# A feed-forward stage computed as seven block products instead of eight, on 1024 tokens at a time

## The reference

```
x = x + layernorm(attention(layernorm(x)))         # one head of width 256, no mask
x = x + layernorm(ffn(layernorm(x)))
ffn(z) = (silu(z @ W_gate.T) * (z @ W_up.T)) @ W_down.T      # W_gate, W_up: 2752 x 1024, W_down: 1024 x 2752
```

## Time and profile before

| | |
|---|---|
| median of 3 runs | 1849.88 us (1849.65 to 1850.52) |
| span of the profiled execution, first to last instruction | 1848.4 us; its own time is not given apart, so the median is 1.5 us above it |
| PE busy | 98% of the span |
| DVE busy | 45% |
| ACT busy | 26% |
| POOL busy | 9% |
| DMA | 199.73 MB, 108 GB/s over the span |
| mean granted clock of TensorE | 0.997 |

### The profile page before, as it was taken

The page is one execution under the profiler, slowest core; times in us unless marked ns, Lnnn a source line. Parts: engine busy times, 40 slices in busy tenths (PEclk is TensorE's granted clock), DMA queues, the critical chain, the costliest instruction groups (busy, mean ns, idle before and its releaser), DMA issues.

```text
span 1848.4 us, 22492 instructions
## 1 busy us (share of the span) xinstructions
PE 1819.5 (98%) x8408; PEld 1511.6 (82%) x8408; DVE 835.0 (45%) x1205; ACT 481.2 (26%) x725; POOL 162.8 (9%) x184
## 2 busy tenths in 40 slices
PE   7999999999999999999999999999999999999997
PEld 5788888888888888888888888888888888888886
DVE  7865766685333442244344423444343234433323
ACT  3233433342222222222222222222222122222221
POOL 4420211221000000011000000110000001000001
PEclk9999999999999999999999999999999999999999
DMA  6311111142222323323324224332232323323231
GB/s 264 114 68 58 45 68 68 68 159 103 101 103 91 136 80 123 128 102 113 125 91 153 74 102 158 114 113 92 110 138 70 146 99 132 113 110 119 98 123 48
DMA packets 36026, 199.73 MB, mean 108 GB/s; under 512 B 4896, under 2 KB 5024, under 8 KB 18848
## 3 DMA queue, kind: packets, MB, share of 16 engines
q1 hardware_dynamic: 36000, 199.39, 29.7%
HBM read 182.59 MB, written 16.79 MB: 108 GB/s over the span
## 4 chain that ended last, share of the span: by engine, by line
PE 95%; DVE 2%; DMA 1%; issue 0%; POOL 0%; ACT 0%; SPq 0%; DVEq 0%; POOLq 0%; ACTq 0%
PE ps L186 29%; PE ps L188 29%; PE ps L187 28%; PE ps L1223 3%; PE ps L1116 2%; PE ps L1224 2%; PE ps L1168 1%; PE ps L1361 1%; PE ps L1169 1%; DVE norm_x_stats L663 0%; DMA x_tile<-x 0%; DMA norm_rows<-stats_dram 0%; DVE xt_f L705 0%; DVE x1n_t L682 0%; ACT xn_t L463 0%
## 5 line engine op out<-in xcount | busy, mean ns | idle before, releaser
L682 DVE TENSOR_TENSOR w_sb<-w_raw,w_sb 128x1024 fp32r<-128x1024 f32 x260 | 309.6, 1230 | 828.3 <-ACT w_sb L521 733.3
L186 PE MATMUL ps<-x1n_t,w_sb 128*128 128x512 f32 x1376 | 535.5, 389 | 0.2 <-DVE x1n_t L682 0.2
L188 PE MATMUL ps<-x1n_t,w_sb 128*128 128x512 f32 x1376 | 535.3, 389 | 0.0
L187 PE MATMUL ps<-x1n_t,w_sb 128*128 128x512 f32 x1376 | 535.3, 389 | 0.0
L521 ACT CAST w_sb<-w_raw 128x1024 fp32r<-128x1024 f32 x248 | 248.2, 1050 | 941.1 <-PE ps L188 909.6
L186 PEld LDWEIGHTS ps<-x1n_t,w_sb 128*128 128x128 f32 x1376 | 258.3, 188 | 54.0 <-issue 0.6
L187 PEld LDWEIGHTS ps<-x1n_t,w_sb 128*128 128x128 f32 x1376 | 258.3, 188 | 53.7
L188 PEld LDWEIGHTS ps<-x1n_t,w_sb 128*128 128x128 f32 x1376 | 258.3, 188 | 53.6
L186 PE MATMUL ps<-w_sb,h_t 128*128 128x512 f32 x672 | 262.6, 391 | 0.0
L188 PE MATMUL ps<-w_sb,h_t 128*128 128x512 f32 x672 | 261.6, 389 | 0.0
L187 PE MATMUL ps<-w_sb,h_t 128*128 128x512 f32 x672 | 261.4, 389 | 0.0
(11 more groups left out here) (117 smaller groups left out, 1703.0 us busy)
## 6 DMA issues: line engine op xcount, KB each, us to landing
w_raw<-wffn SPq DMA_DIRECT2D x124, 1024.0 KB, 4.8
t_tile<-x_dram SPq DMA_DIRECT2D x32, 512.0 KB, 6.5
x_res<-x SPq DMA_DIRECT2D x16, 512.0 KB, 3.3
x_dram<-x_tile SPq DMA_DIRECT2D x16, 512.0 KB, 2.7
out<-y_tile SPq DMA_DIRECT2D x15, 512.0 KB, 2.9
xt_f<-xt SPq DMA_DIRECT2D x6, 1024.0 KB, 8.8
w_raw<-wffn SPq DMA_DIRECT2D x12, 512.0 KB, 3.7
x_rows<-x SPq DMA_DIRECT2D x2, 2048.0 KB, 14.5
```

Of the source, the lines that this page charges most:

```text
L186: pe.matmul(dst, stat(HIGH), mov(HIGH), start=first, stop=False)
L187: pe.matmul(dst, stat(HIGH), mov(LOW), start=False, stop=False)
L188: return pe.matmul(dst, stat(LOW), mov(HIGH), start=False, stop=last)
L682: return dve.tensor_tensor(dst, src, high.bitcast(F32), ALU.subtract)
```

## The change

The feed-forward stage is done in two passes (`PASSES`) over 1024 tokens each. Both of its matrix products are cut into 2 x 2 blocks, and the four block results come from seven block products (`PRODS`) instead of eight, with sums and differences of blocks ahead of and behind them.

- **Tokens.** With A11, A12 (first 512 tokens, the two halves of the 1024 features) and A21, A22 (second 512 tokens): S3 = A11 - A21, S1 = A21 + A22, S2 = A22 - S3, S4 = A12 - S2. POOL makes S3 and S4 (`sum_s3`, `sum_s4`), DVE makes S1 and S2. The seven operands (`xc`) are split into HIGH and LOW and stay in SBUF for the pass; the raw values lie where LOW goes.
- **Weights.** POOL makes four differences for each pair of chunks (`weight_sums`, `last_sum`): TT1, TT3, TT2, TT4.
- **Gate and up.** A pair is two chunks of gate or of up; gate and up pairs take turns, and the last one is mixed. `product` has 4 input chunks x 3 = 12 matmuls; 21 pairs of 7 products per pass. The half chunk is done apart (`rest_first` to `rest_fourth`, 48 matmuls). `post` on DVE adds the products up: 5 additions in a gate pair; 6 operations and 3 multiplications with the gate in an up pair.
- **Hidden values.** After each up pair POOL makes four sums of blocks of h (`hidden_sums`), and SP stores all seven operands to `hsp_dram`, 1.75 MB.
- **Down.** 7 products x 11 steps (`KP`) x 12 matmuls. Each step loads a 256 KB block of h from `hsp_dram` and one of weights (`load_step`, four buffers deep). The differences of W_down are made once, by POOL during attention (`down_sums`), and stored to `wdt_dram`. ACT and DVE copy and add products into `y_all`.
- **Slots.** Every operand block of 128 x 512 is split into one of seven slots; slot n is filled again by n + 7. So a product has one ACT cast and one DVE `low`, a step of down has two.
- **Norm of x1.** For tiles 0 to 11 DVE norms x1 within `attend` (`x1_norm`: two bn_stats, one aggregate, one tensor_scalar), PE transposes it there (`transpose_x1n`, 8 transposes, in tiles t = 4 to 15), ACT copies it out and SP stores it to `xq_dram`. Tiles 12 to 15 are normed during the first gates and transposed in the first down stage (`transpose_tall`).
- The loops are unrolled. At the end, all four tiles of the last product finish in the same step.

The core of the diff (`load_step` on SP, `pair_sums` on POOL, `high` and the end of `attend(t)` on ACT, `product` on PE):

```diff
+            def load_step(P_, s):
+                if s >= 4:
+                    sp.wait_ge(w_low, step_alloc(P_, s - 4) + 2)
...
+                sp.dma_start(w_raw[:, tile, :], hsp_dram[P_, i, k, :, :]).then_inc(d_loaded[s % 4], 16)
...
+                sp.dma_start(w_raw[:, tile + 1, :], part).then_inc(d_loaded[s % 4], 16)
...
+            def pair_sums(P_, p):
+                raw = 4 * pair_buffer(p)
+                pool.wait_ge(w_loaded[pair_buffer(p)], pair_loads(P_, p))
+                if p > 0:
+                    pool.wait_ge(w_low, pair_alloc(P_, p - 1, 3) + 1)
...
+            def high(n):
+                if n >= PASSES * PER:
+                    return
+                if n >= SLOTS:
+                    act.wait_ge(slot_used, n - SLOTS + 1)
...
+                act.copy(slots[:, n % SLOTS, HIGH, :], source(n)).then_inc(w_high, 1)
...
+                if t == TILES - 1:
+                    for n in range(RESTS, SLOTS):
+                        high(n)
+                    split_high(0, A11)
...
+            def product(P_, p, j):
...
+                if j == 4:
+                    pe.wait_ge(e1_done, gp + 1)
+                if j == 5:
+                    pe.wait_ge(u3_done, gp + 1)
+                if j == 6:
+                    pe.wait_ge(c22_done, gp + 1)
+                pe.wait_ge(w_low, n + 1)
+                for c in range(KH):
+                    mm = three(pe, ps[:, 4 * (p % 2) + BANK_OF[j], :], lambda h: slots[:, n % SLOTS, h, cols(c)],
+                               lambda h: xc[XC_OF[j]][:, h, c, :], j < 4 and c == 0, c == KH - 1, j in (0, 1, 3, 4, 5, 6))
+                mm.then_inc(slot_used, 1)
```

More of the change, by code:

```diff
@@ L359, in _ @@
+            gates(1)
+            downs(1)
+            for T in range(2):
+                for i in range(TPB):
+                    store_out(1, T, i)
+            sp.wait_ge(out_stored, 16 * TILES)
         @block.gpsimd
@@ new lines, in gates @@
+            def gates(P_):
+                for p in range(PAIRS):
+                    if p + 1 < PAIRS:
+                        pair_sums(P_, p + 1)
+                    if P_ == 1 and p == 0:
+                        for i in range(1, TPB):
+                            sum_y(0, 1, i)
+                    if p > 0 and is_up(p - 1):
+                        hidden_sums(P_, pair_k(p - 1))
+                    if P_ == 0 and p in (3, 6, 9, 12):
+                        rstd(norm_l, LNT + (p - 3) // 3, 0)
+                hidden_sums(P_, KP - 1)
@@ new lines, in rstd_y @@
+            def rstd_y(P_, T, i):
+                rstd(norm_y, 8 * P_ + 4 * T + i, i)
+            clear_rest(0)
+            gates(0)
+            for h in range(2):
+                sum_s3(1, h)
+            for h in range(2):
+                sum_s4(1, h)
+            rstd_y(0, 0, 0)
+            rstd_y(0, 0, 1)
+            sum_y(0, 0, 0)
+            rstd_y(0, 0, 2)
+            sum_y(0, 0, 1)
+            rstd_y(0, 0, 3)
+            pair_sums(1, 0)
+            rest_sum(1)
+            sum_y(0, 0, 2)
@@ L1016, in y_stats @@
[L1016 to L1030 removed]
+            split_low(0, S1)
@@ L1110, in _ @@
+            y_moments(0, 1, TPB - 1)
+            gates(1)
+            downs(1)
+            for i in range(TPB):
+                y_stats(1, 1, i)
+                if i > 0:
+                    y_norm(1, 1, i - 1)
+                y_moments(1, 1, i)
+            y_norm(1, 1, TPB - 1)
         @block.tensor
@@ new lines, in gates, with transpose_tall @@
+            def gates(P_):
+                for p in range(PAIRS):
+                    for j in range(PRODS):
+                        product(P_, p, j)
+            def transpose_tall(i):
+                if i == 0:
+                    pe.wait_ge(tall_loaded, 16)
+                    pe.wait_ge(c12_done, PAIRS)
+                    pe.wait_ge(silu_done, silu_count(0, MIXED, 1))
+                for g in range(2):
+                    if i > 1:
+                        pe.wait_ge(tall_evicted, 2 * (i - 2) + g + 1)
+                    transposes(2 * (i % 2) + g, KH * g, x1n_tall[:, i, :], KH).then_inc(tall_ready, 1)
@@ L1389 @@
+            gates(0)
+            downs(0)
+            rest_first(1)
+            rest_second(1)
+            rest_third(1)
+            rest_fourth(1)
+            gates(1)
+            downs(1)
 def kernel(**inputs):
```

1321 lines of the change are left out of this document (876 added, 445 removed).

## The result

The changed kernel takes **1765.7 us** (median of 4 runs, 1765.35 to 1766.58), the kernel before took 1850.2 on the same chip: ratio **0.954** [0.953, 0.956]. The forecast was 1727, range 1698 to 1768. The direction and the steady state were right, but the time lies 39 us above the forecast, near the upper edge of the range. The question is thus where 39 of the 123 us of forecast gain went.

What follows compares the result with a forecast made beforehand. PE, busy 98%, was taken as the bound, with matmuls 226.7 ns apart. 1848.4 - 166.8 + 1 + 26 + 6 + 2 + 9.4 = 1726.0, and 1.5 for median above span gives 1727 us; range 1698 to 1768.

Steps and rivals of the forecast that it cites:

- matmuls: Feed-forward stage: 736 fewer matmuls at 226.7 ns each, -166.8 us.
- attention: Attention tiles: x1's added norm work taken as 0, three slots split at the end of t = 14 cost +1 us.
- attention to first pair: Change from attention to feed-forward: waits of 24 us plus 3 of clock, 27 against 0.8, +26 us (+8 to +40).
- steady pairs, down: Gate and up pairs and down steps: other engines and loads keep ahead of PE, 0 us.
- x1n_tall: First down stage of pass 0: PE waits for the 2 MB load at step 4, +6 us (0 to 11).
- between the passes: Start of pass 1: POOL's rest sum and DVE's statistics ahead of the half chunk cost +2 us (0 to 6).
- PE's end to the span's end: Kernel's end: statistics, norms and sums behind the last matmul take 19.5 against 10.1 us, +9.4 (+5 to +13).
- DVE falls behind: Up pairs: POOL's operations meet every DVE split, 20 pairs lose 2.8 us each, +56, 1783 us; 14%.
- bound by its loads: Down: slow load landings make a step take 3.95 us, 154 steps lose 1.23 each, 1916 us; 3%.
- The start is cheap: Attention to feed-forward: sums interleave without waiting, +8 in place of +26, no wait for x1n_tall, 1703 us; 15%.

Runs made afterwards that it cites:

- e13: Changed kernel with added work: POOL makes one sum of h four times more often in the gates, each down step also copies 256 KB DRAM to DRAM; 1778.7 us, single run.
- e3: Changed kernel with the last attention tile's slots split ahead of o_sum and A11's two pieces behind the last probabilities' splits; 1758.9 us.
- e6: On top of e3, POOL makes S3's two pieces ahead of the sum of x1 of tile 14; 1758.9 us.
- e1: Changed kernel with the last y sums of pass 0, and their loads and stores, spread over two pairs of pass 1; 1764.2 us.
- e12: Changed kernel with x1n_tall loaded at step 20, transposed in the third down product, and three y tiles without own residual loads (some outputs not the reference's); 1750.9 us.
- e2: Changed kernel with the half chunk's sum ahead of pair 0's sums and its first product ahead of DVE's statistics, at pass 1's start; 1768.5 us.
- e10: Changed kernel with the order of e2, the half chunk loaded three steps earlier and the third y sum ahead of the pair's; 1763.6 us.
- e5: Changed kernel with POOL's pair 0 sums behind the norm and x1's sum at tile 13, and three slots split ahead of o_sum at tile 14; 1758.1 us.
- e4: Changed kernel with x1n_tall transposed ahead of steps 8 and 9 of the first down product instead of 4 and 7; 1763.6 us.
- e15: Changed kernel, same function, with many queue orders moved together, last y sum on DVE, x1n_tall in the fifth down product; 1732.6 us, ratio 0.936 to before.

## Why the prediction was right, and where it was 39 us short

Idle time is the sum of the brackets above; "slow" is what the starts of neighbouring matmuls lie further apart than 226.7 ns (or a transpose's usual time) without a wait, most of it at half clock, 427 to 430 ns. The slow parts are good to some 0.7 us.

| term | forecast | measured in the trace |
|---|---|---|
| matmuls | -166.8 | count and pitch as forecast |
| attention | +1 | 5.1 idle, and slow 1.9 more than before |
| attention to first pair | 24 idle, 3 of clock | 21.1 idle, 9.3 slow |
| steady pairs, down | 0 | 0 |
| x1n_tall | +6 | 8.5 idle, 2.6 slow |
| between the passes | +2 | 17.3 idle, 6.9 slow |
| PE's end to the span's end | 19.5 | 23.1 |

The excess over forecast is 6 + 3 + 5 + 22 + 4 = 40, against 38.1 found in the span (1764.1 - 1726.0); 2 us are not accounted for.

That the time still lies inside the range is in part luck: the range went up to 1768 for the sake of the rival "DVE falls behind", which was not seen, and the losses that filled it were priced at 2, 6 and 3 us. It lies outside 1712 to 1745, which had 66%.

- **Matmuls, pairs, down:** right. That POOL's 12 operations and DVE's 16 fit in a pair was argued from short durations, and e13 shows room beyond it. DVE came to 11.2 us per pair (212.52 in 360), below the forecast 14. POOL's sums in the gates did lengthen each other and DVE's splits, as the prediction took, and the lead of the slots swallowed it.
- **Attention to first pair:** right in mechanism and, for the idle time, in size: 7.03 (8 forecast), 2.85 (3), 8.84 (9). S4, forecast at 4, cost only 0.52, since 1.83 went to `u3` one product earlier, a wait that the prediction did not have. It gave u3 two products of lead, which the gates kept in steady state; in the first pairs DVE's queue was full, and PE waited ahead of product 5 at 483.98, 1135.25 and 1161.34. e3 showed what holds the last `weigh`, and e6 moved waiting time between S1 and A22. The clock was mis-sized: 3 forecast, 9.3 found. Each of four pauses had matmuls at half clock behind it, and the forecast had added 3 for all of them.
- **Between the passes: the step that failed**, 24.2 in place of 2 (0 to 6). The prediction counted "four pair sums and the norms of y" and DVE's statistics. The step that it left out is SP's residual loads: there is one place for them, thus load, sum, store, load in series, 5 us each, and the sums for pair 2 behind them on POOL. That is 6.78 us of the idle time. e1 and e12 showed that chain (with it taken away, the wait is gone; with only POOL's order changed, it moves to the place where `hs` overlays y). The other 10.5 us are the half chunk's late load, which had no term either, and DVE's queue of statistics, which was counted and priced too low (e2, e10).
- **Attention:** the row for the four down differences was taken as hidden, the *four sums for pair 0* were not looked at: they begin with a wait for a load, in an in-order queue ahead of `rstd`. The three slots of tile 14, priced at 1, cost 2.35. Both taken out of the way in e5: 7.6 us less.
- **x1n_tall:** the load was issued 9.0 us into the stage instead of 7.5 (881.79, the stage's first matmul at 872.76) and landed 10.5 us later instead of 9.5, so the wait was 8.5 instead of 6; the 2.6 of half clock behind it had no term. That another wait would come in its place (e4) was not foreseen; it changed no number of the forecast, but "just transpose it later" gained 2 us instead of 11.
- **The end:** the sums of T = 0 were taken as done. They were not: a norm of DVE from SBUF to SBUF beside a POOL sum took 2.84 (0.80 alone), and the first statistics of T = 1 began 1.8 us after PE's end. Three of the four half norms behind it were each 1.2 longer. This is read from the timeline; no run took it away by itself. With the last sum on DVE (e15) 19.5 were left.
- **The rivals:** "DVE falls behind" and "bound by its loads" were both not seen, and e13 bounds how near they were. "The start is cheap" had the sums interleave; they block each other instead.

## What to carry to other kernels

Follow each in-order queue, the loads' queue too, through every change of stage before pricing it at a few microseconds: here steady state was exact, and the change between two passes, with a chain of single-buffered loads that had not been followed, was missed by 22 us, more than all else together. A wait removed uncovers the next (e1, e4, e6, e10 gave 0 to 2 us each although the wait they aimed at went or shrank); ask what stands next behind it on every engine, and move them together. Price a pause of TensorE together with the half clock behind it: here 52 us of idle time came with some 21 us of slow matmuls.
